# Post-norm vision block on one core: the second attention and the norm behind it, run half by half

## The chip, the cores and the metric

The kernel runs on one core of a Trainium2 chip. The time is the device time of one execution in microseconds (us); the lower, the better. A core has five engines with queues of their own: TensorE (PE in the profile, its weight loads PEld), VectorE (DVE), ScalarE (ACT), GpSimd (POOL) and SyncE (SP, which here only issues transfers). Each works through its own instructions in order and waits for the others at counting semaphores, which the program sets: `wait_ge(sem(name), n)` holds the engine's whole queue until `name` has been raised n times.

## The reference, cut to what matters

Sixteen images of 64 tokens with 64 features pass through a patch embedding, a feed-forward layer, windowed attention with 8 heads, a feed-forward layer, a second attention with one head and a distance bias, a layer norm, and then a block with an RMS norm, rotary attention, an RMS norm and a mixture of 8 experts, and a last layer norm. The change touches the second attention, the layer norm behind it and the RMS norm that opens the next block:

```python
# second attention (one head of 64, bias from two cosines of |i-j| weighted by beta), h3 is its input
q = h3 @ Wq.T + bq; k = h3 @ Wk.T + bk; v = h3 @ Wv.T + bv
o2 = softmax(q @ k.T / 8 + bias) @ v
h4 = layernorm(h3 + o2)                       # (x - m) / sqrt(var + 1e-5)
# third attention opens with an RMS norm of h4, then keys and queries with rotary tables
n = h4 * rsqrt(mean(h4 * h4) + 1e-6) * ln1_w
q3 = rope(n @ wq.T); k3 = rope(n @ wk.T); v3 = n @ wv.T
```

## The kernel before, in words

All activations stay in SBUF. The 1024 tokens stand as 128 rows by 512 columns (two groups of 8 images side by side in the rows). Nearly every step is done twice, once for each half of the columns (g = 0 and g = 1, 256 columns, `HC`), so that one engine can work on one half while the next engine has the other. PSUM is one array of 8 banks, `PS[:, bank, :]`, and half g of the second attention uses banks 4g to 4g+3.

The order of the work is written out by hand, once per engine. In the second attention and the norm behind it each engine does a step for both halves before it goes to the next step:

- TensorE (`block.tensor`, lines 443 to 500): queries and keys (L447, L448) of halves 0 and 1; for each half the bias by a product with the identity (L453) and 8 score products (L459, 64x64 tiles, 16 instructions in the trace); `turn2(0)` (two transposes, L440), the values of both halves (L317), `turn2(1)`; h3 turned and centred for both halves (L470); mixing for both halves (L481); then `stay_awake(15, 1)`, 15 products of zeros into bank 1 whose result nobody reads (L279); the transposes of the normed activations h4n of both halves (L490); and the keys, turned keys, queries and turned queries of the third attention for half 0 and half 1 (L497). Behind them come `values3(0)` (L317 again), a mask product (L505) and `scores3` (L511).
- VectorE (`block.vector`, lines 1155 to 1211): keys' bias (L1157) for both halves, top and shift of the scores (L1162, L1164) for both, values' bias (L1168) for both, reciprocals (L1173), o2 (L1178), sum2 (L1184), sums of squares (L1014), reciprocals of the RMS norm's roots and the scaling to h4n (L1020, L1025), the same for the layer norm (h4), and then the rotary products (L1203) and sums (L1210).
- ScalarE (`block.scalar`, lines 795 to 825): q2 (L799) for both halves, probabilities by Exp (L803) for both, a table load for Sqrt (`bring_table`, L713), squares (L726) for both, roots for the RMS norm (L811) and the layer norm (L719) for both, h4f (L818) for both, a table load for Exp, and the key heads of the third attention (L823).
- GpSimd has nothing in this stretch. Its next work is the sum for q3 (L949). Further on, at the second RMS norm, it takes inverse roots itself: L954 adds the epsilon to 128x4 sums, and L956 raises them to the power -0.5.

h4 (the layer norm's result) is read late, by `open3` and `residual`, behind the third attention's first scores. h4n is read by L490 at once.

Of the kernel before, what the change touches and what calls it, by code (L numbers as in the profile page):

```python
# [30 lines left out]
D = 64  # L31
# [54 lines left out]
def build(nc, x, pack_a, pack_b, pack_c, pack_d, pack_e, out):  # L86
    with ExitStack() as ctx:
# [182 lines left out]
        def _(pe):  # L270
# [172 lines left out]
            pe.wait_ge(sem("pack_c_loaded"), 16)  # L443
            for g in range(2):
                pe.wait_ge(sem("h3_ready"), g + 1)
                cols = slice(g * HC, (g + 1) * HC)
                mm(PS[:, 4 * g, 0:HC], c("aq"), h3[:, cols], start=True, stop=True).then_inc(sem("q2_mm"), 1)  # L447
                mm(PS[:, 4 * g + 1, 0:HC], c("ak"), h3[:, cols], start=True, stop=True).then_inc(sem("k2_mm"), 1)  # L448

            pe.wait_ge(sem("bias_made"), 2)  # L450
            for g in range(2):
# [10 lines left out]
            turn2(0)  # L462
            pe.wait_ge(sem("v2_centred"), 2)
            for g in range(2):
                values(h3, c("av"), D, 4 * g + 2, g).then_inc(sem("v2_mm"), 1)
            turn2(1)

            for g in range(2):
# [4 lines left out]
            for g in range(2):  # L473
# [11 lines left out]

            stay_awake(15, 1)
            for g in range(2):
# [5 lines left out]
            for g in range(2):  # L493
                pe.wait_ge(sem("h4f_ready"), g + 1)
                cols = slice(g * HC, (g + 1) * HC)
                for n, name in enumerate(("fk", "fk_turned", "fq", "fq_turned")):
                    t = mm(PS[:, 1 + 4 * g + n // 2, (n % 2) * HC:(n % 2 + 1) * HC], c(name), h4f[:, cols],  # L497
# [3 lines left out]


# [205 lines left out]
        def _(act):  # L708
# [13 lines left out]
            def squares_of(name, ready, count, src):  # L722

                for g in range(2):
                    act.wait_ge(sem(ready), count[g])
                    f(half(squares, g), half(src, g), ACT.Square).then_inc(sem(name + "_squared"), 1)  # L726

# [66 lines left out]

            act.wait_ge(sem("bias_made"), 2)
            for g in range(2):
                act.wait_ge(sem("q2_mm"), g + 1)

# [6 lines left out]

            bring_table(ACT.Sqrt)
            squares_of("ln1", "ln1_in", (1, 2), sum2)
            for g in range(2):
                at = slice(4 * g, 4 * g + 4)
                act.wait_ge(sem("ln1_sq_sum"), g + 1)  # L810
                f(std_rms[:, at], sq_sums[:, at], ACT.Sqrt, scale=(1.0 + EPS_RMS) / D, bias=const(EPS_RMS * EPS))\  # L811
                    .then_inc(sem("rms1_std"), 1)
            roots("ln1", std, 1.0 / D, EPS)


# [3 lines left out]
            bring_table(ACT.Exp)  # L819
# [125 lines left out]


# [47 lines left out]
        def _(ve):  # L994
# [160 lines left out]
            for g in range(2):  # L1155
                ve.wait_ge(sem("k2_mm"), g + 1)
                v.tensor_scalar(half(k2, g), PS[:, 4 * g + 1, 0:HC], c("abk"), None, ALU.add).then_inc(sem("k2_dve"), 1)  # L1157
            for g in range(2):
# [7 lines left out]
            for g in range(2):  # L1166
# [3 lines left out]
            for g in range(2):  # L1170
                mixed2 = PS[:, 4 * g + 2, 0:4 * (D + 1)].rearrange("q (t d) -> q t d", d=D + 1)
                ve.wait_ge(sem("att2_mixed"), g + 1)
                v.reciprocal(r2[:, 4 * g:4 * g + 4], mixed2[:, :, D]).then_inc(sem("att2_recip"), 1)  # L1173
            for g in range(2):
                ts = slice(4 * g, 4 * g + 4)
                mixed2 = PS[:, 4 * g + 2, 0:4 * (D + 1)].rearrange("q (t d) -> q t d", d=D + 1)
# [3 lines left out]
            for g in range(2):  # L1180
# [6 lines left out]
            for g in range(2):  # L1187
                sum_squares("ln1", g)
            for g in range(2):
                invert("rms1", g, rstd_rms, std_rms)  # L1190
                scale("rms1", g, h4n, sum2, rstd_rms).then_inc(sem("h4n_ready"), 1)
            for g in range(2):
                invert("ln1", g, rstd, std)
            for g in range(2):
# [277 lines left out]
```

## Time and profile before

| | us |
|---|---|
| median of 3 runs | 130.06 |
| lowest, highest | 129.52, 131.12 |
| the profiled execution | 130.09 |
| its span, first to last instruction | 128.3 |
| TensorE, VectorE, ScalarE, GpSimd busy in it | 114.1, 85.2, 62.8, 16.9 |
| mean granted TensorE clock | 0.993 of full speed |

The span is what the trace covers; 1.8 us of the profiled execution's time lie around it. A step that ends the chain later moves the time by the same amount as the span.

### The profile page before, as it was taken

Reading aid. Unit: us, or ns where it says so; the run is one execution under the profiler, and the core shown is the slowest. Engines: PE = TensorE matmul, PEld = TensorE weight load, DVE = VectorE, ACT = ScalarE, POOL = GpSimd, SP = SyncE. Lnnn points to the kernel's source line nnn. Section 1 sums busy time; section 2 is a strip of 40 time slices with the busy share of each in tenths; the row PEclk is TensorE's granted clock in tenths of the full one; section 3 lists DMA queues with packets and bytes.
Section 4 is the critical chain, followed back from the end, with each engine's and each line's share of the span. In section 5 each row is a group of like instructions: output and inputs, shape, how many; then the busy total and the mean of one; then the engine's idle time right before and its main releaser. Section 6 shows DMA issues by size and latency. Waiting matters only on the chain.

```text
span 128.3 us, 2347 instructions
## 1 busy us (share of the span) xinstructions
PE 114.1 (89%) x912; PEld 75.3 (59%) x919; DVE 85.2 (66%) x181; ACT 62.8 (49%) x124; POOL 16.9 (13%) x40
## 2 busy tenths in 40 slices
PE   5999999969999989999999996999999999799630
PEld 2334564737687764795686884878768772224330
DVE  0000599799996354558798644487599949999960
ACT  4000668965132175655853647573575646443040
POOL 7300009300000000000022003270013400000000
PEclk9999999999999999999999999999999999999997
DMA  4999980000000000000000000000000000000003
GB/s 156 331 391 432 418 331 2 0 0 0 5 0 3 5 0 0 3 0 5 0 0 0 5 0 0 5 0 0 0 0 0 0 0 3 0 0 5 0 0 82
DMA packets 2682, 6.99 MB, mean 55 GB/s; under 512 B 1264, under 2 KB 1392, under 8 KB 2544
## 3 DMA queue, kind: packets, MB, share of 16 engines
q1 hardware_dynamic: 2672, 6.86, 14.1%
q8 instruction: 7, 0.11, 0.4%
q14 instruction: 3, 0.02, 0.1%
HBM read 6.59 MB, written 0.26 MB: 53 GB/s over the span
## 4 chain that ended last, share of the span: by engine, by line
PE 59%; DVE 17%; DMA 7%; issue 6%; ACT 4%; POOL 2%; SPq 2%; POOLq 1%; ACTq 0%
DMA shared_x<-x_dram 7%; PE PS L395 5%; PE PS L627 5%; PE PS L628 5%; PE PS L309 4%; PE PS L511 3%; PE PS L381 3%; PE PS L635 3%; PE PS L298 3%; PE PS L372 3%; PE PS L497 3%; DVE shared_x L1338 3%; DVE shared_h L1268 2%; PE PS L405 2%; PE PS L317 2%
## 5 line engine op out<-in xcount | busy, mean ns | idle before, releaser
L1268 DVE TENSOR_TENSOR shared_h<-PS,shared_f 128x512 f32<-128x512 f32 x22 | 14.9, 682 | 5.3 <-ACT shared_f L880 5.2
L627 PE MATMUL PS<-xf,up_hi 128*128 128x512 f32 x44 | 17.8, 404 | 0.3 <-DVE shared_h L1268 0.3
L628 PE MATMUL PS<-xf,up_lo 128*128 128x512 f32 x44 | 17.4, 396 | 0.0
L880 ACT ACTIVATE shared_f<-PS 128x512 f32<-128x512 f32 x22 | 12.9, 595 | 7.3 <-PE PS L628 7.3
L279 PE MATMUL PS<-idle_bf 128*128 128x512 bf16 x34 | 10.7, 438 | 1.8 <-POOL idle_bf L911 1.3
L1104 DVE TENSOR_REDUCE top<-PS 128x8 f32<-128x512 f32 x12 | 8.3, 689 | 2.6 <-PE PS L511 1.2
L627 PEld LDWEIGHTS PS<-xf,up_hi 128*128 128x128 f32 x44 | 8.3, 188 | 2.7 <-DVE shared_h L1268 0.9
L1030 DVE TENSOR_SCALAR kf<-PS,pack_a_sb 128x256 f32<-128x256 f32 x1 | 0.5, 484 | 13.4 <-PE PS L287 13.4
L713 ACT ACT_TABLE_LOAD x7 | 9.0, 1283 | 0.8 <-PEq L1463 0.7
L785 ACT ACTIVATE probs<-PS 128x512 f32<-128x512 f32 x8 | 4.8, 597 | 9.3 <-PE PS L381 9.3
L628 PEld LDWEIGHTS PS<-xf,up_lo 128*128 128x128 f32 x44 | 8.3, 188 | 1.8
L635 PE MATMUL PS<-shared_h,down_w 128*64 128x512 f32 x32 | 8.2, 611 | 1.2 <-DVE shared_h L1330 1.2
L1106 DVE TENSOR_TENSOR shifted<-PS,top 128x512 f32<-128x512 f32 x12 | 8.3, 691 | 0.4
L279 PEld LDWEIGHTS PS<-idle_bf 128*128 128x128 bf16 x39 | 3.8, 106 | 7.5 <-issue 4.0
L287 PE MATMUL PS<-shared_x 128*64 128x256 f32 x48 | 7.4, 435 | 0.3 <-DMA shared_x<-x_dram 0.3
L395 PE MATMUL PS<-vo,probs 128*64 128x18 f32 x128 | 7.2, 214 | 0.0
L395 PEld LDWEIGHTS PS<-vo,probs 128*64 128x64 f32 x128 | 6.4, 137 | 1.2 <-issue 1.2
L949 POOL TENSOR_TENSOR qf<-shared_f 128x256 f32<-128x256 f32 x2 | 1.4, 724 | 43.0 <-DVE shared_f L1203 43.0
L901 ACT ACTIVATE up_w<-PS 128x512 f32<-128x512 f32 x8 | 4.3, 595 | 5.3 <-PE PS L650 5.3
L381 PE MATMUL PS<-pack_a_sb,shifted 128*128 128x128 f32 x32 | 5.2, 285 | 1.2 <-DVE shifted L1106 1.2
L381 PEld LDWEIGHTS PS<-pack_a_sb,shifted 128*128 128x128 f32 x32 | 3.4, 140 | 3.9 <-DVE shifted L1106 3.3
L740 ACT ACTIVATE kf<-PS,pack_a_sb 128x256 f32<-128x256 f32 x1 | 0.5, 473 | 10.8 <-PE PS L287 10.8
(189 smaller groups left out, 217.4 us busy)
## 6 DMA issues: line engine op xcount, KB each, us to landing
shared_x<-x_dram SPq DMA_DIRECT2D x6, 544.0 KB, 6.8
up_w<-pack_d_dram SPq DMA_DIRECT2D x1, 1408.0 KB, 12.5
pack_c_sb<-pack_c_dram SPq DMA_DIRECT2D x1, 796.5 KB, 13.3
pack_b_sb<-pack_b_dram SPq DMA_DIRECT2D x1, 455.0 KB, 9.6
down_w<-pack_e_dram SPq DMA_DIRECT2D x1, 352.0 KB, 13.5
out_dram<-normed SPq DMA_DIRECT2D x4, 64.0 KB, 1.7
pack_a_sb<-pack_a_dram SPq DMA_DIRECT2D x1, 162.0 KB, 9.0
```

Source lines behind the costliest of these rows:

```text
L279: mm(PS[:, bank, 0:cols], idle_bf[:, 0:P], idle_bf[:, 0:cols], start=True, stop=True)
L287: m = mm(PS[HALF * s:HALF * s + HALF, 4 + g, 0:HC], x_sb[:, k, 2 * COLS:XW], x_sb[:, k, first:first + HC], start=(k == 0), stop=(k == KCH ...
L381: t = tp(PS[:, w % 2, ch * P:(ch + 1) * P], shifted[:, w % 2, ch * P:(ch + 1) * P], ident)
L395: t = mm(PS[r, 4 + w // 4, at:at + wide], probs[:, w % 2, col:col + HALF], vo[:, w % 2, (w // 2) * 2 + s, ch].rearrange("q e d -> q (e d)" ...
L627: mm(up, up_hi[:, at:at + P], moving, start=True, stop=False)
L628: mm(up, up_lo[:, at:at + P], moving, start=False, stop=True).then_inc(sem("up_mm"), 1)
L635: t = mm(PS[HALF * s:HALF * s + HALF, bank, tok], down_w[:, DOWN_AT[ch]:DOWN_AT[ch] + D], hh[:, ch, s, tok], start=True, stop=True)
L713: f(table_use[:, :], const(1.0), func)
L880: f(gate[:, n % UPBUF, :], PS[:, UP_BANKS[n % UPBUF][0], :], ACT.Silu).then_inc(sem("gated"), 1)
L1104: v.reduce_max(tops, rows, AX).then_inc(sem(name + "_top"), 1)
L1106: v.tensor_tensor(shifted[:, n % 2, :].rearrange("q (b h n) -> q b h n", b=2, n=N), rows, tops.unsqueeze(3).to_broadcast([P, 2, 4, N]), AL ...
L1268: v.tensor_tensor(hh[:, ch, :, g * HC:(g + 1) * HC], PS[:, UP_BANKS[n % UPBUF][1], :].rearrange("q (s c) -> q s c", s=2), gate[:, n % UPBU ...
```

## The change

Each engine's work on the second attention and the norm is put into functions of one half, and the halves are run some steps apart. The roots and reciprocals of the two norms (two Sqrt activations and two reciprocals for each half) go to GpSimd, which does a multiply-and-add and a power for each norm and half; ScalarE's table loads for Sqrt and back to Exp go with them, and the load for Exp is asked for ahead of q2. `squares_of` is removed. Of the products of zeros, 11 remain in four places.

```diff
 TensorE
-            for g in range(2):
...
-            turn2(0)
-            pe.wait_ge(sem("v2_centred"), 2)
-            for g in range(2):
-                values(h3, c("av"), D, 4 * g + 2, g).then_inc(sem("v2_mm"), 1)
-            turn2(1)
...
-            stay_awake(15, 1)
...
+            pe.wait_ge(sem("pack_c_loaded"), 16)
+            pe.wait_ge(sem("bias_made"), 2)
+            queries_keys2(0)
+            pe.wait_ge(sem("v2_centred"), 2)
+            values(h3, c("av"), D, 2, 0).then_inc(sem("v2_mm"), 1)
+            scores2(0)
+            turn_h3(0)
+            queries_keys2(1)
+            turn2(0)
+            values(h3, c("av"), D, 6, 1).then_inc(sem("v2_mm"), 1)
+            mix2(0)
+            scores2(1)
+            turn_h3(1)
+            stay_awake(1, 1)
+            turn2(1)
+            stay_awake(2, 1)
+            mix2(1)
+            stay_awake(7, 1)
+            turn_h4(0)
+            stay_awake(1, 5)
+            queries_keys3(0)
+            turn_h4(1)
+            queries_keys3(1)
 ScalarE
+            bring_table(ACT.Exp)
             act.wait_ge(sem("bias_made"), 2)
             for g in range(2):
...
             for g in range(2):
                 act.wait_ge(sem("att2_turned"), g + 1)
                 f(p2[:, 2 * g:2 * g + 2, :], PS[:, 4 * g + 1, 0:HC].rearrange("q (u n) -> q u n", n=P),
                   ACT.Exp).then_inc(sem("att2_probs"), 1)
-            bring_table(ACT.Sqrt)
-            squares_of("ln1", "ln1_in", (1, 2), sum2)
-            for g in range(2):
...
-            roots("ln1", std, 1.0 / D, EPS)
+                if g == 0:
+                    act.wait_ge(sem("ln1_in"), 1)
+                    f(half(squares, 0), half(sum2, 0), ACT.Square).then_inc(sem("ln1_squared"), 1)
+            act.wait_ge(sem("ln1_in"), 2)
+            f(half(squares, 1), half(sum2, 1), ACT.Square).then_inc(sem("ln1_squared"), 1)
             for g in range(2):
...
-            bring_table(ACT.Exp)
 GpSimd
+            for g in range(2):
+                at = slice(4 * g, 4 * g + 4)
+                pool.wait_ge(sem("ln1_sq_sum"), g + 1)
+                g_.tensor_scalar(std_rms[:, at], sq_sums[:, at], (1.0 + EPS_RMS) / D, EPS_RMS * EPS, ALU.mult, ALU.add).then_inc(sem("ln1_above"), 1)
+                pool.wait_ge(sem("ln1_above"), 2 * g + 1)
+                g_.tensor_tensor(rstd_rms[:, at], std_rms[:, at], minus_half[:, at], ALU.pow).then_inc(sem("rms1_rstd"), 1)
+                g_.tensor_scalar(std[:, at], sq_sums[:, at], 1.0 / D, EPS, ALU.mult, ALU.add).then_inc(sem("ln1_above"), 1)
+                pool.wait_ge(sem("ln1_above"), 2 * g + 2)
+                g_.tensor_tensor(rstd[:, at], std[:, at], minus_half[:, at], ALU.pow).then_inc(sem("ln1_rstd"), 1)
 VectorE
...
+            keys2(0)
+            values2(0)
+            shift2(0)
+            keys2(1)
+            values2(1)
+            residual1(0)
+            sum_squares("ln1", 0)
+            shift2(1)
+            scale("rms1", 0, h4n, sum2, rstd_rms).then_inc(sem("h4n_ready"), 1)
+            residual1(1)
+            scale("ln1", 0, h4, sum2, rstd)
+            sum_squares("ln1", 1)
+            scale("rms1", 1, h4n, sum2, rstd_rms).then_inc(sem("h4n_ready"), 1)
+            scale("ln1", 1, h4, sum2, rstd)
```

On VectorE `keys2(g)` is L1157, `shift2(g)` L1162 and L1164, `values2(g)` L1168, and `residual1(g)` L1173, L1178 and L1184 in one. On TensorE `queries_keys2(g)` is L447 and L448, `scores2(g)` L453 and L459, `turn_h3(g)` L470, `mix2(g)` L481, `turn_h4(g)` L490 and `queries_keys3(g)` L497, each for one half.

## Rows read from the trace of the kernel before

**Rows 1.** The page: the span, and the chain that ended last, by engine.

```profile
span 128.3 us, 2347 instructions
...
PE 59%; DVE 17%; DMA 7%; issue 6%; ACT 4%; POOL 2%; SPq 2%; POOLq 1%; ACTq 0%
```

**Rows 2.** The chain of waits from 50 to 68 us: start us, us, what.

```profile
50.59 0.63 PE PS L447 x2
...
52.51 0.43 PE PS L453 x2
...
53.55 0.63 PE PS L453 x2
...
54.79 0.37 PE PS L440 x2
...
56.06 0.22 PE PS L440 x2
...
57.17 1.10 PE PS L481 x32
...
58.30 0.18 DVE r L1173
...
59.49 0.43 ACT squares L726
...
61.48 0.44 DVE kf L1025
...
61.96 0.44 PE PS L490 x2
...
62.41 3.72 PE PS L497 x16
...
66.74 1.02 PE PS L511 x16
```

**Rows 3.** The timeline of the same stretch: start us, us, engine, line, operation.

```profile
51.31 0.47 ACT L799 ACTIVATE qf<-PS,q_bias 128x256 f32<-128x256 f32 x1 [1.43 <-PE PS L447]
...
55.20 0.38 ACT L803 ACTIVATE p<-PS 128x256 f32<-128x256 f32 x1 [1.31 <-PE PS L440]
...
56.71 1.28 ACT L713 ACT_TABLE_LOAD   x1
...
58.01 0.20 ACT L713 ACTIVATE table_use<-consts 128x1 f32<-128x1 f32 x1
...
58.41 3.19 PE L279 MATMUL PS<-idle_bf 128*128 128x512 bf16 x14 [0.16 <-issue]
...
62.93 1.28 ACT L713 ACT_TABLE_LOAD   x1
63.58 0.76 DVE L1203 TENSOR_TENSOR shared_f<-PS,pack_c_sb 128x256 f32<-128x256 f32 x2 [0.80 <-PE PS L497]
...
65.55 0.72 POOL L949 TENSOR_TENSOR qf<-shared_f 128x256 f32<-128x256 f32 x1 [41.93 <-DVE shared_f L1203]
```

**Rows 4.** The timeline at the second RMS norm, where GpSimd takes the roots.

```profile
76.81 0.42 DVE L1014 TENSOR_REDUCE sq_sums<-squares 128x4 f32<-128x256 f32 x1 [1.07 <-ACT squares L849]
...
77.32 0.23 POOL L954 TENSOR_SCALAR std_rms<-sq_sums 128x4 f32<-128x4 f32 x1 [9.26 <-DVE sq_sums L1014]
...
77.62 1.04 POOL L956 TENSOR_TENSOR rstd_rms<-std_rms,minus_half 128x4 f32<-128x4 f32 x1
```

**Rows 5.** The timeline where VectorE and GpSimd read SBUF at one time, late.

```profile
84.71 1.04 POOL L960 CAST pick<-pack_c_sb 128x1024 fp32r<-128x1024 f32 x1
...
84.96 1.07 DVE L1225 TENSOR_TENSOR parts<-normed,parts 128x256 f32<-128x256 f32 x1
```

**Rows 6.** GpSimd's own timeline, early, the copy of 8 columns.

```profile
19.64 2.90 POOL L938 CAST router_parts<-router_s 128x8 fp32r<-128x8 f32 x1
```

**Rows 7.** VectorE's own timeline at the same time, an operation with two inputs in SBUF.

```profile
19.33 3.15 DVE L1057 SCALAR_TENSOR_TENSOR up_lo<-up_w,pack_a_sb,up_hi 128x2816 fp32r<-128x2816 f32 x1
```

**Rows 8.** A window of 1 us with little TensorE work: PE, PEld, DVE, ACT, POOL busy, PEclk.

```profile
109.00:110.00 1.00, 0.04 (x2) 0.05 (x2) 1.00 (x3) 0.85 (x2) 0.00 (x0) 1.00 0.00 0
```

More of the change, by code:

```diff
@@ L461, in _, with turn_h3 @@
                 t.then_inc(sem("att2_scores"), 1)
-            turn2(0)
-            pe.wait_ge(sem("v2_centred"), 2)
-            for g in range(2):
-                values(h3, c("av"), D, 4 * g + 2, g).then_inc(sem("v2_mm"), 1)
-            turn2(1)
-            for g in range(2):
+            def turn_h3(g):
                 for u in (2 * g, 2 * g + 1):
@@ L472, in _, with mix2 @@
                 t.then_inc(sem("h3_turned"), 1)
-            for g in range(2):
+            def mix2(g):
                 pe.wait_ge(sem("v2_ready"), g + 1)
@@ L483, in _, with turn_h4 @@
                 t.then_inc(sem("att2_mixed"), 1)
-            stay_awake(15, 1)
-            for g in range(2):
+            def turn_h4(g):
                 pe.wait_ge(sem("h4n_ready"), g + 1)
@@ L491, in _, with queries_keys3 @@
                 t.then_inc(sem("h4_turned"), 1)
-            for g in range(2):
+            def queries_keys3(g):
                 pe.wait_ge(sem("h4f_ready"), g + 1)
-                cols = slice(g * HC, (g + 1) * HC)
                 for n, name in enumerate(("fk", "fk_turned", "fq", "fq_turned")):
-                    t = mm(PS[:, 1 + 4 * g + n // 2, (n % 2) * HC:(n % 2 + 1) * HC], c(name), h4f[:, cols],
+                    t = mm(PS[:, 1 + 4 * g + n // 2, (n % 2) * HC:(n % 2 + 1) * HC], c(name), half(h4f, g),
                            start=True, stop=True)
@@ L720, in roots @@
                         .then_inc(sem(name + "_std"), 1)
[L722 to L726, printed above, removed]
             def gelus(name, u_banks):
@@ L1152, in _, with keys2, shift2 @@
                                        in1=half(h2, g), op0=ALU.add, op1=ALU.add).then_inc(sem("h3_ready"), 1)
-            for g in range(2):
+            def keys2(g):
                 ve.wait_ge(sem("k2_mm"), g + 1)
                 v.tensor_scalar(half(k2, g), PS[:, 4 * g + 1, 0:HC], c("abk"), None, ALU.add).then_inc(sem("k2_dve"), 1)
-            for g in range(2):
+            def shift2(g):
                 ts = slice(4 * g, 4 * g + 4)
@@ L1165, in _, with values2 @@
                                 ALU.subtract).then_inc(sem("att2_shifted"), 1)
-            for g in range(2):
+            def values2(g):
                 ve.wait_ge(sem("v2_mm"), g + 1)
@@ L1169, in _, with residual1 @@
                                 c("abv").unsqueeze(1).to_broadcast([P, 4, D]), ALU.add).then_inc(sem("v2_ready"), 1)
-            for g in range(2):
+            def residual1(g):
+                ts = slice(4 * g, 4 * g + 4)
                 mixed2 = PS[:, 4 * g + 2, 0:4 * (D + 1)].rearrange("q (t d) -> q t d", d=D + 1)
                 ve.wait_ge(sem("att2_mixed"), g + 1)
[L1173 to L1176, printed above, removed]
+                v.reciprocal(r2[:, ts], mixed2[:, :, D]).then_inc(sem("att2_recip"), 1)
                 ve.wait_ge(sem("att2_recip"), g + 1)
@@ L1184, in _ @@
                 v.tensor_tensor(half(sum2, g), PS[:, 4 * g + 3, 0:HC], half(o2, g), ALU.add).then_inc(sem("ln1_in"), 1)
[L1187 to L1194, printed above, removed]
-                scale("ln1", g, h4, sum2, rstd)
+            keys2(0)
[12 more added lines that the diff above has]
+            scale("ln1", 1, h4, sum2, rstd)
             cos = c("rope_cos").unsqueeze(1).to_broadcast([P, 4, N])
```

15 lines of the change are left out of this document (4 added, 11 removed).

## The prediction

> **What bounds the kernel now.** I read the page first: the span is 128.3 us, and the chain that ended last is TensorE for 59% and VectorE for 17% of it [rows 1]. Then I read the chain in order of time around the change, 50 to 68 us [rows 2]. It falls into two parts. From 50.59 to 58.27 TensorE runs without a gap: queries, keys, bias, scores, values and mixing for both halves, each wait of the others covered by the other half's products. From 58.30 to 62.41 the chain leaves TensorE: reciprocal, o2, sum2, squares (59.49), sums, roots, scaling to h4n (half 1's at 61.48), the transposes at 61.96, and at 62.41 the keys and queries of the third attention. In that time TensorE multiplies zeros (14 recorded products from 58.41, 3.19 us, 0.23 each) [rows 3]. Last I read the timeline at 63 to 67 us, for what waits behind: VectorE's rotary products start at 63.58, GpSimd's sum for q3 runs from 65.55 to 66.27 [rows 3], and the scores that need it start at 66.74, because TensorE arrives only then [rows 2]. So VectorE has 66.74 - 66.27 = 0.47 us to spare there, about 0.42 after a handover.
>
> So what the change can win is the 4.1 us of the tail, and it should be judged by when the *second* half leaves it, since the third attention's order needs both halves soon after one another.
>
> **The change part by part.** I lay out the new order with the old durations. The trace gives: 0.43 for a product of 256 columns, 0.63 where it follows 64x64 tiles (52.51 against 53.55), 0.61 for the scores of one half (54.79 - 53.55 - 0.63), 0.22 for two transposes, 0.37 behind tiles and 0.44 on an idle engine, 0.45 for half the values or half of the turned h3 (0.90 between the rows at 54.79 and 56.06, and 0.89 between 56.28 and 57.17, are both halves), 0.55 for mixing one half [rows 2]. A step of VectorE or ScalarE on 128x256 that waits for the one before it takes 0.45 in all (59.49 to 59.94), a reciprocal 0.2 [rows 2], Exp 0.38 [rows 3].
>
> *TensorE, first half.* From 50.59: queries and keys (0.63 + 0.43) to 51.65, values to 52.10, bias and scores to 53.14, turned h3 (0.45 and 0.2 for the change of tile) to 53.79, queries and keys of half 1 to 54.65, turn2(0) to 54.87, values of half 1 to 55.32, mixing of half 0 (0.55) to 55.87. VectorE has half 0's shift done at 54.1 (two steps behind 53.14) and ScalarE's Exp ends at 55.3, both in time. Half 0 is mixed at 55.87, and before that took until about 57.7: 1.8 us earlier.
>
> *TensorE and VectorE, second half.* Bias and scores of half 1 (0.63 + 0.61) end at 57.11, turned h3 at 57.76, one product of zeros at 57.99. VectorE meanwhile does residual1(0): reciprocal, o2, sum2 from 55.9 to 57.0; then `sum_squares("ln1", 0)` waits for ScalarE's square (57.45) and runs to 57.9. Behind that waiting instruction stand the top and shift of half 1, whose scores are there since 57.11; TensorE's turn2(1), Exp, mix2(1) all wait for them. So top and shift end at 58.8 and not at 58.1, and turn2(1) (0.44 on an idle engine) ends at 59.25, Exp at 59.67, mixing at 60.3, where both halves were mixed at 58.27 before [rows 2]: the second half is 2.0 us late. This is the first step that speaks against the change.
>
> *GpSimd's roots.* At the second RMS norm the sum of squares ends at 77.23, GpSimd's add starts at 77.32 (0.23), the power at 77.62 (1.04) and ends at 78.66: 1.43 us from the sums to the inverse root [rows 4]. The old way, root and reciprocal, took 0.55 (60.37 to 60.92, between the rows of rows 2). So every norm and half costs 0.9 more, and the layer norm's follows the RMS norm's in GpSimd's queue: add, handover and power, 1.34 more. The new add also multiplies; no row shows that form, and I bound it by 0.23 (same shape, one operation) and 0.74 (the 0.72 of the sum for q3 on 256 columns, rows 3); I take 0.23, the row of its own shape. The power has no cost of a first call, as its row above was its first.
>
> *The two halves through the tail.* Half 0: sums at 57.9, inverse root at 59.3, h4n at 59.8, against about 61.36 before (half 1's scaling started at 61.48 behind it). Half 1: mixing 60.3, residual1(1) to 61.4, squares and sums to 62.3, root at 63.73, h4n at 64.17, where it was ready at 61.92 [rows 2]: 2.25 us later. The layer norm's root of half 1 comes at 65.07. `scale("ln1", 1)` waits for it, and it stands in VectorE's queue *ahead* of the rotary products, which have nothing to do with it. They start one step later, at about 65.45, where it was 63.58 [rows 3] (pitch 0.35 to 0.38 for two neighbours that do not depend, 0.76 for two). That is 1.87 later, less 0.42 to spare: **+1.45 us** at the scores.
>
> *TensorE's own path.* The seven zero products behind mix2(1) (7 x 0.23) end at 61.9, turn_h4(0) at 62.2, h4f at 62.75 (ScalarE has it behind the square of half 1, which ends at 61.85), and the keys and queries of half 0 run from 62.75 to 64.6 (half of 3.72) and not from 62.41. turn_h4(1) now stands behind them and h4f(1) behind that: 0.22 + 0.5 in which TensorE is idle, where before it ran through. It ends at 67.3 and not at 66.13, +1.15. This is less than VectorE's +1.45, so VectorE's path sets the end. Half 0's head start is lost here: it leaves the tail at 59.8 and is not used before 62.
>
> *Table loads.* The loads at 56.71 and 62.93 (1.28 each) lay beside ScalarE's waiting [rows 3] and win nothing. The new load for Exp starts when ScalarE falls free at 49.88 (51.31 - 1.43) and delays q2(0) to 51.4 to 51.9; TensorE asks for it at 52.10. Cost 0; without that cover (the values ahead of the bias) it would be 0.25. In the trace the use of a table starts 1.30 us after the load does (56.71, 58.01) [rows 3]. The Trainium skill, page "ScalarE: Activation LUTs", section "What ACT_TABLE_LOAD costs", gives 2.66 us for a switch, a drain included; by it q2(0) would be ready at 53.2 and the change would lose another 1.1 us at the scores. The row decides, and I leave it out.
>
> *The reads that VectorE and GpSimd share.* A copy of 8 columns on GpSimd took 2.90 us, from 19.64 to 22.54, beside a VectorE operation with two inputs in SBUF that ended at 22.48 [rows 6, 7]; and a VectorE subtraction with two inputs in SBUF took 1.07 us beside a GpSimd copy that ended at 85.75, 0.28 before it [rows 5], where the same shape takes 0.43 (the scaling of rows 2). So each can hold up the other. The scaling to h4n reads sum2 and the roots, both in SBUF, at the moment when GpSimd starts the layer norm's add. If the add goes first, h4n is 0.2 late; if the scaling then holds the power, the layer norm's root is 0.3 late: +1.75 in place of +1.45. Below, it costs nothing. I take 0.1, nearer to nothing, since GpSimd reads only 4 columns.
>
> Sum: 1.45 + 0.1 = 1.55 on the profiled execution's 130.09 (span 128.3 and 1.8 around it; 0.03 above the median): **131.6 us**. Behind the scores the order is the old one and has no transfer or clock of its own to catch up with, so nothing gives the 1.55 back.
>
> **The rivals.** *The interleaving delivers, no slower than before.* My layout holds half 1 for 0.7 at the sum of squares and charges 0.2 at three changes of tile; if these cost nothing, half 1 is mixed at 59.0. This decides it: TensorE's path is then at -0.15, VectorE's at +0.15, less if the power's 1.04 is partly the engine's own record (its spans are rough). For it: half 0 is 1.8 us earlier and the tail holds no useful TensorE work. Against it: the chain for half 1 is one of dependent steps with durations from rows. 129.9 to 130.5, say 130.2.
>
> *GpSimd holds VectorE through add and power.* If the scaling to h4n has to wait for the whole pair, 1.3 us [rows 4], it does so in both halves. In half 0 it ends at 60.9 and not at 59.8, and residual1(1) starts 0.6 late. In half 1 h4n ends at 66.0: turn 0.44, h4f 0.5, keys and queries to 68.9 or 69.0, +2.8. That gives 132.9. For it: rows 5 to 7. Against it: there is a gap of 0.07 between add and power [rows 4], in which the waiting scaling gets in. The Trainium skill, page "SBUF — State Buffer", section "SBUF: two separate sides", states an exclusive lock for the whole instruction between a VectorE operation with two SBUF inputs and a GpSimd operation that reads SBUF. By that rule, held by one instruction at a time, the sum would be the +1.75 above.
>
> *TensorE's clock falls.* TensorE idles for some 0.8 us before turn2(1) and 0.5 at two more places. For it: more gaps than before. Against it: in the window from 109 us it was busy for 0.04 of 1 us and the granted clock stayed at 1.00, the level of 2.4 GHz [rows 8]. If it fell to 1.2 GHz, the keys' and queries' products alone (3.72) would cost 3.7 more: 135.3.
>
> **How the numbers follow.** Forecast 0.63, interleaving delivers 0.20, GpSimd holds VectorE 0.12, clock 0.05. The forecast's own range is 131.1 to 132.2 (handovers and the 0.3 of the shared reads). The range of 8 in 10 reaches to the rivals on both sides: 130.0 to 132.9. What a measurement of this kernel can tell from no change is about 2%, 2.6 us: above 132.7 lie the clock case and most of the held case, 0.12; below 127.5 only something that I do not see, 0.03; within, 0.85.
>
> **What would show it.** In the profile of the changed kernel: half 0's mixing ends near 55.9 and half 1's near 60.3; VectorE is idle ahead of its sum of squares and TensorE ahead of turn2(1) by some 0.8; the four powers take 1.04 each; h4n of half 1 is ready near 64.2; VectorE waits for GpSimd ahead of h4's second scaling until 65, the rotary products start near 65.4, and the third attention's first scores near 68.2. I am wrong if half 1 is mixed before 59.3, if the rotary products start before 64.3, or if the scores' start moves by less than 0.8 us; a scaling of 1 us or more would speak for the held pair, and a granted clock under 1.00 between 57 and 68 for the last rival.

## The result, and the profile after

The changed kernel takes 133.09 us (median of 4 runs, 132.72 to 133.94) against 130.59 for the kernel before beside it: a ratio of 1.0239, with a 95% interval of 1.0195 to 1.0282. Measured again in a later session it took 132.59 us against 130.21, a ratio of 1.0175 (1.0147 to 1.0204). It is slower by 2.4 to 2.5 us, where 1.55 were forecast, and its median lies just above the range. One execution of run 3 below (136.04 us) was over 1.5% slower than the fastest of its kernel; the ratio in the table leaves it out, the median does not.

| | before | after |
|---|---|---|
| the profiled execution, us | 130.09 | 133.94 |
| its span | 128.3 | 131.9 |
| time outside the span | 1.8 | 2.0 |
| first q2 product to first scores of the third attention | 16.15 | 18.37 |

The last row is the measure for all that follows: the start of the first score products of the third attention minus the start of the first product for q2, 66.74 - 50.59 in [rows 2]. It leaves out how early the input arrived, and the granted clock is 1.00 all through it, in every trace but one.

The page of the changed kernel: the span, the granted clock in forty slices, and the chain that ended last, by engine.

```profile
span 131.9 us, 2342 instructions
...
PEclk9999999999999999999999999599999999999997
...
PE 63%; DVE 19%; issue 6%; POOL 5%; ACT 4%; POOLq 1%; ACTq 0%; DVEq 0%
```

GpSimd now has 5% of the chain, where it had 2% [rows 1]. One slice, at 82.4 to 85.7 us, shows the clock at 0.5; that comes below. The chain of waits of the changed kernel (start us, us, what):

```profile
50.74 0.63 PE PS L445 x2
...
55.48 0.12 issue
55.59 0.70 PE PS L474 x16
...
58.38 0.34 DVE s_top L1173
...
58.75 0.43 DVE s_shift L1175
...
59.23 0.44 PE PS L440 x2
59.67 0.43 PE PS L279 x2
...
60.23 0.70 PE PS L474 x16
...
60.95 0.20 DVE r L1187
...
62.16 0.43 ACT squares L816
...
62.61 0.43 DVE sq_sums L1024
...
63.12 0.21 POOL std_rms L950
...
63.40 1.01 POOL rstd_rms L952
...
64.49 0.44 POOL std L953
...
65.00 1.02 POOL rstd L955
...
66.04 0.42 DVE h L1035
66.46 0.68 DVE shared_f L1216 x2
...
68.33 0.74 POOL qf L959
...
69.11 1.09 PE PS L524 x16
```

Read against [rows 2]. Half 0's mixing (55.59) ends at 56.29, 2.0 us before both halves were mixed in the kernel before (58.27). But the chain does not follow half 0. It goes from half 0's sum of squares (which holds VectorE) to half 1's top and shift at 58.38, over the turn, the Exp (beside it the two zero products) and half 1's mixing, which ends at 60.93. Then it passes through residual, squares and sums to GpSimd at 63.12, and stays on GpSimd through *both* norms (63.12 to 66.02). The layer norm's scaling (66.04) and the rotary products (66.46) follow, and then the scores at 69.11. In the timeline, for the same stretch:

```profile
59.82 0.42 DVE L1035 TENSOR_TENSOR kf<-h,rstd_rms 128x256 f32<-128x256 f32 x1 [0.65 <-POOL rstd_rms L952]
59.87 0.43 POOL L953 TENSOR_SCALAR std<-sq_sums 128x4 f32<-128x4 f32 x1
...
63.32 1.99 PE L487 MATMUL PS<-h,pack_c_sb 128*128 128x256 f32 x8 [0.35 <-ACT h L819]
...
64.44 0.43 DVE L1035 TENSOR_TENSOR kf<-h,rstd_rms 128x256 f32<-128x256 f32 x1 [1.41 <-POOL rstd_rms L952]
64.49 0.43 POOL L953 TENSOR_SCALAR std<-sq_sums 128x4 f32<-128x4 f32 x1
...
65.57 0.47 ACT L819 ACTIVATE h<-PS,pack_c_sb 128x256 f32<-128x256 f32 x1 [2.30 <-PE PS L481]
66.04 0.42 DVE L1035 TENSOR_TENSOR h<-h,rstd 128x256 f32<-128x256 f32 x1 [1.18 <-POOL rstd L955]
...
66.09 1.99 PE L487 MATMUL PS<-h,pack_c_sb 128*128 128x256 f32 x8 [0.57 <-ACT h L819]
```

TensorE's own path: keys and queries of half 0 (the eight products at 63.32), those of half 1 from 66.09, behind a turn and h4f(1) at 65.57. Before, one block of 3.72 began at 62.41 [rows 2].

### The profile page after: what moved, and what is told of

The parts are those of the page before. It is cut to its first block, busy times and chain, and to the rows that moved or that the text cites. A ratio compares the mean times of both kernels' runs of the same rounds, so it can differ in the third digit from the quotient of the medians.

```text
span 131.9 us, 2342 instructions
## 1 busy us (share of the span) xinstructions
PE 116.9 (89%) x915; PEld 76.5 (58%) x915; DVE 85.1 (65%) x177; ACT 59.1 (45%) x117; POOL 23.0 (17%) x48
## 4 chain that ended last, share of the span: by engine, by line
PE 63%; DVE 19%; issue 6%; POOL 5%; ACT 4%; POOLq 1%; ACTq 0%; DVEq 0%
PE PS L287 5%; PE PS L395 5%; PE PS L640 5%; PE PS L279 5%; PE PS L641 4%; PE PS L309 4%; PE PS L524 3%; PE PS L381 3%; PE PS L648 3%; PE PS L298 3%; PE PS L372 3%; DVE shared_x L1351 3%; PE PS L405 2%; DVE shared_h L1281 2%; ACT shared_f L880 2%
## 5 line engine op out<-in xcount | busy, mean ns | idle before, releaser
L279 PE MATMUL PS<-idle_bf 128*128 128x512 bf16 x35 | 11.8, 438 | 1.3 <-POOL idle_bf L911 1.3
L1024 DVE TENSOR_REDUCE sq_sums<-squares 128x4 f32<-128x256 f32 x8 | 3.4, 420 | 3.8 <-ACT squares L849 1.6
```

What stands on the lines that cost most here:

```text
L279: mm(PS[:, bank, 0:cols], idle_bf[:, 0:P], idle_bf[:, 0:cols], start=True, stop=True)
```

## The experiments

Fourteen runs were made; run 9 is the changed kernel once more. "Path" is the 16.15 or 18.37 of the table above, "outside" the time outside the span in all runs of the kernel.

| run | median us | before beside it | ratio (95%) | path | outside |
|---|---|---|---|---|---|
| 1 h4 late | 132.37 | 130.16 | 1.0166 (1.0101 to 1.0231) | 17.96 | 1.98 to 2.06 |
| 2 no power | 132.71 | 130.16 | 1.0188 (1.0138 to 1.0239) | 17.96 | 1.98 to 2.05 |
| 3 power only | 134.92 | 130.16 | 1.0317 (1.0237 to 1.0397) | 20.85 | 2.01 to 2.05 |
| 4 shift first | 132.16 | 130.16 | 1.0160 (1.0111 to 1.0209) | 17.74 | 1.99 to 2.06 |
| 5 old roots | 131.47 | 130.09 | 1.0096 (1.0066 to 1.0125) | 17.57 | 1.74 to 1.82 |
| 6 after, zeros in the gap | 132.44 | 130.09 | 1.0166 (1.0130 to 1.0201) | 18.37 | 1.99 to 2.08 |
| 7 before, zeros in the gap | 130.13 | 130.09 | 0.9992 (0.9972 to 1.0012) | 16.15 | 1.75 to 1.83 |
| 8 half tail | 130.06 | 130.09 | 1.0020 (0.9985 to 1.0054) | 16.14 | 1.75 to 1.82 |
| 9 change again | 132.59 | 130.21 | 1.0175 (1.0147 to 1.0204) | 18.37 | 2.03 to 2.06 |
| 10 both moves | 132.29 | 130.21 | 1.0150 (1.0121 to 1.0179) | 17.42 | 1.99 to 2.12 |
| 11 split pairs | 130.76 | 130.21 | 1.0047 (1.0015 to 1.0080) | 16.81 | 1.76 to 1.83 |
| 12 half tail, 8 zeros | 129.85 | 130.21 | 0.9978 (0.9953 to 1.0004) | 15.87 | 1.74 to 1.82 |
| 13 side powers | 130.70 | 130.14 | 1.0054 (1.0021 to 1.0087) | 16.32 | 2.02 to 2.10 |
| 14 side adds | 130.10 | 130.14 | 0.9980 (0.9958 to 1.0002) | 16.15 | 1.76 to 1.83 |

### 1. The layer norm's scaling out of VectorE's way

```diff
             scale("rms1", 1, h4n, sum2, rstd_rms).then_inc(sem("h4n_ready"), 1)
-            scale("ln1", 1, h4, sum2, rstd)
...
                 t.then_inc(sem("rope_q"), 1)
+                if g == 0:
+                    scale("ln1", 1, h4, sum2, rstd)
```

> The changed kernel, with the layer norm's scaling of half 1 (scale of ln1, 1) moved from ahead of the rotary products to between the rotary products of half 0 and half 1. Theory A (VectorE's queue is held by that scaling, which waits for GpSimd's second power of half 1 until 66.02, and TensorE's own path ends 0.5 to 0.6 us before it): the rotary products start about 1.2 us earlier, near 65.2, but the third attention's first scores only 0.5 to 0.6 us earlier, near 68.5 and not 69.11, because TensorE ends the keys and queries of half 1 at 67.9; 0.5 to 0.6 us less than the changed kernel, so about 2.0 us over the kernel before. Theory B (VectorE alone sets the end): 1.2 us less. Theory C (the wait on VectorE is hidden anyway): no change, 2.5 us over the kernel before.

The path is 17.96, 0.41 less than the change's. The chain now runs over TensorE:

```profile
63.21 2.00 PE PS L487 x8
65.21 0.23 PE PS L481 x2
...
65.46 0.48 ACT h L819
...
65.99 2.00 PE PS L487 x8
...
68.59 1.02 PE PS L524 x16
```

Keys and queries of half 0, the turn, h4f(1), keys and queries of half 1, values, mask, scores: behind half 1's mixing no wait for VectorE or GpSimd is left. So VectorE's queue did set the end (theory A, not C), and TensorE's path was 0.4 us behind it (not B's 1.2).

### 2. GpSimd's power taken away

```diff
-                g_.tensor_tensor(rstd_rms[:, at], std_rms[:, at], minus_half[:, at], ALU.pow).then_inc(sem("rms1_rstd"), 1)
+                g_.tensor_tensor(rstd_rms[:, at], std_rms[:, at], minus_half[:, at], ALU.mult).then_inc(sem("rms1_rstd"), 1)
...
-                g_.tensor_tensor(rstd[:, at], std[:, at], minus_half[:, at], ALU.pow).then_inc(sem("ln1_rstd"), 1)
+                g_.tensor_tensor(rstd[:, at], std[:, at], minus_half[:, at], ALU.mult).then_inc(sem("ln1_rstd"), 1)
```

> The changed kernel with GpSimd's four powers behind the first norm replaced by products of the same operands and shape, so that the norm's factor is another number; all waits and the order stay. It takes the price of the power alone away. Theory A: a product takes 0.2 to 0.3 us and not 1.01, so h4n of half 1 comes 0.8 us earlier and the rotary products 1.5 us earlier, but turn_h4(1) stands behind queries_keys3(0), which ends at 65.2 in both, so TensorE's path stays and the first scores start 0.5 to 0.6 us earlier as in the run before this: 2.0 us over the kernel before. Rival (the powers are the whole loss): 1.6 us less, 0.9 us over the kernel before.

The path is 17.96 again, to the hundredth the same as in run 1, though the products that stand for the powers took 0.20 to 0.26 and h4n of half 1 was there at 63.99. The rival's 1.6 is out. Two different edits that end in one figure show the same bound behind them: TensorE's order.

### 3. The power alone, in the old order

The roots go to GpSimd as in the change, and nothing else is touched:

```diff
-            for g in range(2):
-                at = slice(4 * g, 4 * g + 4)
-                act.wait_ge(sem("ln1_sq_sum"), g + 1)
-                f(std_rms[:, at], sq_sums[:, at], ACT.Sqrt, scale=(1.0 + EPS_RMS) / D, bias=const(EPS_RMS * EPS))\
-                    .then_inc(sem("rms1_std"), 1)
-            roots("ln1", std, 1.0 / D, EPS)
...
```

> The kernel before, its order unchanged, with the roots and reciprocals of the first norm moved to GpSimd as in the change, and the table loads for Sqrt and Exp gone with them. Theory A: GpSimd's queue does the RMS norm and the layer norm of half 0 (2.9 us) before it starts half 1, h4n of half 1 is ready near 65.2 and not 61.9, both transposes stand ahead of the keys and queries on TensorE, and these start 3 us later: 3.0 us over the kernel before, more than the whole change. Rival (the roots are not what costs, the half-by-half order is): less than 1 us over the kernel before.

Path 20.85, 4.7 over the kernel before. In the chain, GpSimd does RMS norm and layer norm of half 0 and then the RMS norm of half 1, one behind the other:

```profile
60.42 0.20 POOL std_rms L940
...
60.70 1.04 POOL rstd_rms L942
...
61.82 0.44 POOL std L943
...
62.33 1.01 POOL rstd L945
...
63.42 0.20 POOL std_rms L940
...
63.70 1.02 POOL rstd_rms L942
...
65.22 0.44 PE PS L490 x2
65.66 5.14 PE PS L497 x16
```

The keys and queries begin at 65.66 and not at 62.41: 3.25 later, where 3.0 were expected. The block then takes 5.14 and not 3.72, which was not expected: from 61.6 to 65.2 TensorE had only two transposes to do, and the granted clock stood at 0.50 from 65.6 to 69. So in the old order GpSimd's roots cost 3.3 us and in this profile the clock 1.4 more. The other executions took 133.25 to 136.04 us, so the clock's share differs from one to the next. In the change GpSimd's work of half 0 (58.48 to 61.39) is over before half 1's sums are there; here it stands ahead of half 1.

### 4. Half 1's shift ahead of half 0's sum of squares

```diff
-            sum_squares("ln1", 0)
             shift2(1)
+            sum_squares("ln1", 0)
+            residual1(1)
             scale("rms1", 0, h4n, sum2, rstd_rms).then_inc(sem("h4n_ready"), 1)
-            residual1(1)
```

> The changed kernel with VectorE's order changed in two places: top and shift of half 1 ahead of the sum of squares of half 0, and residual1(1) ahead of the scaling of half 0 to h4n. Theory A (half 1 is held by the wait for ScalarE's square in VectorE's queue): mixing of half 1 ends 0.8 us earlier, near 60.1 and not 60.93, and all behind it: 0.5 to 0.8 us less than the changed kernel, 1.8 us over the kernel before. Rival (the half-0 chain matters as much, its roots come 0.4 us later): no change.

Mixing of half 1 ends at 60.13 and the path is 17.74, 0.63 less. The wait of VectorE for ScalarE's square, with half 1's finished scores behind it, was a real cost, near the 0.7 of the forecast. The second move in the edit keeps half 0's scaling, whose root now comes at 60.11, out of half 1's way; no run parts the two. One more row of this run is used below: here GpSimd's add for half 0's layer norm has no scaling of VectorE beside it.

```profile
60.19 0.19 POOL L953 TENSOR_SCALAR std<-sq_sums 128x4 f32<-128x4 f32 x1
```

### 5. The order with the old roots

ScalarE's Sqrt and VectorE's reciprocals come back, in the order of run 4 (with one more move: half 1's sum of squares ahead of the layer norm's scaling of half 0); GpSimd has nothing in this stretch. The cut is shown against run 4.

```diff
             shift2(1)
             sum_squares("ln1", 0)
             residual1(1)
+            invert("rms1", 0, rstd_rms, std_rms)
             scale("rms1", 0, h4n, sum2, rstd_rms).then_inc(sem("h4n_ready"), 1)
...
+            bring_table(ACT.Sqrt)
...
+            roots1(0)
             act.wait_ge(sem("ln1_in"), 2)
             f(half(squares, 1), half(sum2, 1), ACT.Square).then_inc(sem("ln1_squared"), 1)
+            features4(0)
+            roots1(1)
+            features4(1)
+            bring_table(ACT.Exp)
```

> The half-by-half order of the change with shift2(1) and residual1(1) moved ahead as in the fourth run, but the roots on ScalarE (Sqrt, its table loaded behind the second Exp) and the reciprocals on VectorE, as in the kernel before; GpSimd has nothing here. It parts the order from GpSimd's roots. Theory A (both cost: GpSimd's latency, and the order, which leaves TensorE idle at half 1's shift and at its turn_h4): h4n of half 1 is ready near 63.7, and TensorE's keys and queries of half 1, behind those of half 0 and one turn, end near 67.4; first scores near 68.0, 0.4 us before the fourth run and 1.3 us behind the kernel before. Rival (the order is sound and GpSimd is all of the loss): the first scores at 66.7 or earlier, no slower than the kernel before.

Path 17.57; 1.4 us over the kernel before, with no GpSimd in it at all. So the order by itself costs more than half of the change's 2.2 us on the path, and the rival (only GpSimd costs) falls. Its chain shows where: half 1's top and shift (57.39 to 58.28) and its turn and Exp (58.33 to 59.2) are dependent steps with too little of TensorE's work left to put beside them, and from 64.82 to 65.60 TensorE does nothing but half 1's turn (0.23) and then waits for h4f.

```profile
57.39 0.44 DVE s_top L1178
...
57.85 0.44 DVE s_shift L1180
...
58.33 0.44 PE PS L440 x2
...
59.33 0.70 PE PS L474 x16
...
62.82 2.00 PE PS L487 x8
64.82 0.23 PE PS L481 x2
...
65.07 0.48 ACT h L826
...
65.60 1.99 PE PS L487 x8
```

### 6, 7 and 9. The clock

Two of the change's first four runs had a mean granted clock of 0.98, and 133.17 and 133.94 us. In the profiled one of them the fall lies behind the gap of 1.2 us ahead of L405, which both kernels have (in the kernel before from 78.6 to 79.8, with the clock at 1.00). Windows of 1 us of the changed kernel (PE, PEld, DVE, ACT, POOL busy, PEclk):

```profile
82.00:83.00 1.00, 0.75 (x14) 0.75 (x16) 0.53 (x2) 0.02 (x1) 0.00 (x0) 0.66 0.00 0
83.00:84.00 1.00, 1.00 (x12) 0.88 (x9) 0.00 (x0) 0.39 (x1) 0.00 (x0) 0.50 0.00 0
84.00:85.00 1.00, 1.00 (x7) 1.00 (x5) 0.57 (x2) 0.38 (x1) 0.00 (x0) 0.50 0.00 0
85.00:86.00 1.00, 1.00 (x5) 0.87 (x4) 0.49 (x2) 0.39 (x1) 0.00 (x0) 0.64 0.08 16
```

The clock stood at 0.50, the level of 1.2 GHz. L405, L574 and L566 there take 1.10, 1.04 and 0.85 in the chain; the same steps in the kernel before (L405, L561, L553), at 1.00, the level of 2.4 GHz, take 0.68, 0.59 and 0.61. With the two products behind them that is about 1.2 us. Run 6 fills this gap in the changed kernel, run 7 in the kernel before:

```diff
             mix3(3)
+            stay_awake(5, 5)
             mixed_to_features("att3", 7, 1)
```

> The changed kernel with five products of zeros into bank 5, which is free there, ahead of mixed_to_features(att3, 7, 1): they stand in TensorE's gap of 1.2 us at 81 to 82.2, behind which the granted clock showed 0.50 for 3.5 us in the changed kernel's profile. Theory D (this gap, and nothing of the change's own stretch, lets the clock fall in some runs, which costs 1.2 us in each of them): no run shows the clock under 1.00 between 82 and 86, runs lie within 0.5 us of each other and the median falls by 0.3 to 0.8 us, to 2.2 us over the kernel before. Rival (the fall follows the thinner stretch at 58 to 66 of the change): it stays in half of the runs.

> The same five products of zeros in the kernel before, as a control; its profile had the same gap at 78.6 to 79.8 with the clock at 1.00. Theory D: runs that fall there are few in the kernel before, so the time is the same to 0.3 us, and its slowest runs (131 us) go. Rival (the fall belongs to the change alone): no run of either kernel without the change ever shows it, no difference at all.

Of the five executions of run 6 four lie within 0.33 us, and the median is 132.44. The fifth, 133.18, is the one with a profile: in it the fall at 82 is gone, and one stands in another place, from 113.8 to 117.2, late in the experts' part. Run 7 changes nothing (0.9992). Run 9 is the unchanged change:

> The changed kernel once more, beside the kernel before in the same session, as the measure for the three that follow and for the first four runs. All theories: 2.4 to 2.9 us over the kernel before, and in about half of the runs a mean granted clock of 0.98 with a time some 0.5 to 1 us above the others.

This time no run lay more than 0.3 us above the others, at 132.36 to 132.65, and the clock in the profile is at 1.00 to the end of TensorE's work. So in one and the same kernel the fall comes in one execution and stays away in another. In the two sessions the medians of the change differ by 0.5 us, but those of the kernel before beside it differ by 0.4 (130.59 and 130.21), so the distance between the two kernels hardly moved: 2.50 and 2.38. The mean clock alone does not tell what a fall costs: in run 9 an execution of 132.53 us has 0.983. Run 6, with the gap filled, is at 2.35. Filling it won nothing that these runs can tell.

The gap stands in all fourteen profiles in which it is not filled, at 1.19 to 1.21 us. The clock falls behind it in five of them: the change, runs 2 and 4, and runs 13 and 14 below, which leave the order and the roots of the kernel before as they are. The clock in run 14's page, in forty slices of 3.2 us:

```profile
PEclk9999999999999999999999999599999999999985
```

So the fall does not need the new order. All five have GpSimd's added instructions, as have four of the nine without a fall; with one profile for each run that is too few to say whether they have a part in it. What tips it is open.

### 10. Both moves together

The edits of runs 1 and 4.

> The two moves of the first and fourth runs together (layer norm's scaling of half 1 behind the rotary products of half 0; shift2(1) ahead of the sum of squares and residual1(1) ahead of the scaling of half 0), GpSimd's powers kept. Theory A (then TensorE's path alone binds: the keys and queries of half 0, one turn, h4f, those of half 1): first scores 17.4 us behind the first product for q2, against 18.4 in the change and 17.6 with the old roots, so GpSimd's powers cost nothing once no queue waits for them; 1.3 us over the kernel before. Rival (each power on the path keeps its price): as in the fourth run, 17.7 and 1.8 us over the kernel before.

The first product for q2 and the first scores in its chain:

```profile
50.72 0.63 PE PS L445 x2
...
68.14 1.02 PE PS L524 x16
```

Path 17.42, by 0.15 *shorter* than with the old roots (17.57), which have a reciprocal of 0.2 on VectorE ahead of half 0's scaling. In the chain of run 10 there is no GpSimd between 50 and 68 us. So GpSimd's 1.01 per power costs nothing here as soon as no queue waits for it; the 2.2 us of the change are 0.95 of queue order on VectorE (of which 0.41 go away with the powers too, in run 2) and 1.27 of TensorE's order. The time (132.29) came out 0.5 above what path and outside give (1.27 + 0.25 over 130.21 is 131.7); its profile has a fall of the clock from 113 to 116.4, which may be worth about that; in the other three executions a fall is only supposed.

### 11. TensorE's order mended

Run 5 with the turn of half 1 between the keys and the queries of half 0 (`pair3(g, 0)` is the keys and turned keys of half g, `pair3(g, 1)` its queries):

```diff
-            queries_keys3(0)
-            turn_h4(1)
-            queries_keys3(1)
+            pair3(0, 0)
+            turn_h4(1)
+            pair3(0, 1)
+            pair3(1, 0)
+            pair3(1, 1)
```

> The fifth run's kernel (half-by-half order, old roots), with turn_h4(1) moved from behind the keys and queries of half 0 to between its keys and its queries, so that ScalarE's h4f(1) runs beside the queries. Theory A (TensorE's idle 0.8 us at that turn is one part of the order's loss): the gap goes, first scores near 16.8 to 16.9 us behind the first product for q2 and not 17.6, 0.6 to 0.7 us over the kernel before. Rival (the fill and drain of the split pairs take it back, or the rotary products set the end): 17.4 or more.

Path 16.81, 0.76 less: TensorE's idle time at that turn is gone, and 130.76 us remain, 0.55 over the kernel before.

### 8 and 12. What half a tail is worth in the old order

The kernel before, with TensorE's scores of both halves together as they were, and half 0 let through first: `mix2(0)` ahead of `turn_h3(0)` and `turn2(1)`, `residual1(0)` and its sum of squares ahead of half 1's, the RMS norm's root of half 0 ahead of half 1's square, the turn of half 1 between keys and queries of half 0, and the layer norm's scalings behind the rotary products of half 0 and behind `shift3(1)`.

```diff
             for g in range(2):
                 values(h3, c("av"), D, 4 * g + 2, g).then_inc(sem("v2_mm"), 1)
+            mix2(0)
+            turn_h3(0)
             turn2(1)
+            turn_h3(1)
+            mix2(1)
...
-            stay_awake(15, 1)
+            stay_awake(11, 1)
...
```

> The kernel before, with what the first runs suggest: TensorE keeps scores of both halves together and mixes half 0 as soon as its values and probabilities are there; VectorE does residual, squares' sum and scaling for half 0 ahead of half 1; roots stay on ScalarE; TensorE turns h4n of half 1 between the keys and the queries of half 0; the layer norm's scalings stand behind the rotary products of half 0 and behind shift3(1). Theory A: mixing of half 0 ends near 56.7 and of half 1 near 58.5, keys of half 0 start near 61.8 and not 62.4, and the third attention's first scores 0.3 to 0.5 us earlier, near 66.3; 0.3 to 0.5 us less than the kernel before. Rival (TensorE's work is one block behind the later half whatever the order): same time as the kernel before to 0.2 us.

No gain (path 16.14): h4n(0) was ready at 60.85 but stood behind the products of zeros, of which 11 were too many. Run 12 has 8 in their place.

> The eighth run's kernel with 8 products of zeros ahead of turn_h4(0) and not 11. In the eighth run h4n of half 0 was ready at 60.85 and TensorE turned it at 61.2 to 61.4, behind the products of zeros. Theory A (these held the path): h4f(0) and the keys of half 0 0.35 to 0.5 us earlier, first scores 15.8 us behind the first product for q2 and not 16.15, 0.3 to 0.4 us less than the kernel before. Rival (the later half holds TensorE whatever comes ahead): no difference.

Path 15.87, keys of half 0 from 61.89. 129.85 us against 130.21, the lowest median of all kernels; but the interval (0.9953 to 1.0004) still holds 1, so it beats the change surely and the kernel before only by the trace. Its chain now goes over ScalarE's table load for Sqrt (L722, 1.28 us from 58.48), which the kernel before hid: here GpSimd's roots might have a place. No run tries it.

### 13 and 14. What lies outside the span

In every run of every kernel with GpSimd's roots 1.98 to 2.12 us lay outside the span, and 1.74 to 1.84 in every other. Run 13 puts the eight GpSimd instructions into the kernel before, on tiles that nobody reads; run 14 only the four multiply-and-adds.

```diff
+            for g in range(2):
+                at = slice(4 * g, 4 * g + 4)
+                pool.wait_ge(sem("ln1_sq_sum"), g + 1)
+                for n in range(2):
+                    g_.tensor_scalar(side[:, at], sq_sums[:, at], (1.0 + EPS_RMS) / D, EPS_RMS * EPS, ALU.mult, ALU.add).then_inc(sem("side_above"), 1)
+                    pool.wait_ge(sem("side_above"), 2 * g + n + 1)
+                    g_.tensor_tensor(side_root[:, at], side[:, at], minus_half[:, at], ALU.pow).then_inc(sem("side_done"), 1)
+                    pool.wait_ge(sem("side_done"), 2 * g + n + 1)
```

> The kernel before, with the change's eight GpSimd instructions (four multiply-and-adds, four powers) added at the same place on tiles that nobody reads; roots stay on ScalarE. Nobody waits for them. Theory E (the eight instructions by themselves lengthen the part of the time outside the span, which was 1.98 to 2.12 us in every run of a kernel that has them and 1.74 to 1.83 in every other): outside the span 2.0 to 2.1, 0.25 us over the kernel before; first scores 16.15 us behind the first product for q2 as before, up to 0.3 later if VectorE's scalings are held up. Rival (what lies outside the span follows the removed table loads or the other order, not these instructions): 1.75 to 1.83 outside the span, no change in the time.

> The same with the four multiply-and-adds alone, no powers. Theory E with the cost by the number of GpSimd's instructions: between 1.83 and 2.0 outside the span. Rival (it comes with the powers): 1.75 to 1.83; rival (it is a step that comes with any): 2.0 to 2.1.

Run 13: 2.02 to 2.10 in all ten runs. Run 14: 1.76 to 1.83 in all eleven. So the 0.25 comes with the added instructions and not with the table loads that went. Run 2, with products for powers, had it too (1.98 to 2.05), so it isn't the power. Four multiply-and-adds don't bring it and eight instructions do; since the four that run 14 lacks are also the ones with two input tensors, the runs don't tell the number from the kind. What happens there, before the first or behind the last recorded instruction, no trace shows; that it goes by the length of GpSimd's program is a supposition. In run 13 the sum for q3 starts only at 66.01, behind the last power, and the path is 0.17 longer: the eight instructions are not quite free, though nobody reads their results.

## Why the prediction was wrong in size

The direction, the place and the order of the bounds held; the size did not: 1.55 us forecast, 2.4 to 2.5 measured. On the path it is 2.22 for 1.55: 0.59 from the second half's sums, 0.14 from the shared reads, less 0.07 for a shorter root, and 0.02 behind the rotary products; each is taken up below. Then 0.25 lie outside the span. And the kernel before, from whose 130.09 us the forecast was counted, stood at 130.59 beside the change. Together that is 133.06; the median was 133.09.

*TensorE, first half.* The forecast had half 0 mixed 5.28 us behind the first q2 product (55.87); it was 5.55. One half's mixing by itself takes 0.70 and stands 0.12 behind its waits, where half of the pair's 1.10 had been put in. This is the first mis-sized term, and half 1's mixing pays it again.

*TensorE and VectorE, second half.* The hold at `sum_squares("ln1", 0)` is there (run 4: 0.63). Half 1 was mixed 10.19 us behind the first product, forecast 9.71. Of these 0.48, 0.27 are carried on from half 0; nearly all the rest is half 1's own mixing, 0.84 from the Exp's end (60.09) to 60.93 for 0.63. The residual then took 1.21 and not 1.1. Together the sums of half 1 were 0.59 later than forecast: **the failed step is the layout of the second half through mixing and residual**, in which durations of steps that ran in pairs were halved or taken without their handovers.

*GpSimd's roots.* 1.36 us from the sums (63.04) to the root (64.40), forecast 1.43; the new add with its product took 0.20, near the 0.23 taken from the row of its own shape.

*The shared reads.* Forecast 0.1, measured 0.24. The layer norm's add took 0.43 beside VectorE's scaling, which reads two tensors in SBUF, at 59.87 and 64.49 in the timeline above, and ended just behind it. In run 4, where no such instruction of VectorE ran beside it, half 0's took 0.19 (at 60.19). GpSimd waited and VectorE did not (the scaling kept its 0.42 to 0.43), so the held rival (h4n at 66.0) did not come: h4n(1) was there at 64.87. That the rival's 132.9 lies near the measured 133.09 is chance. The other direction is in run 13: there GpSimd's sum for q3 (66.01, 0.72) began just before VectorE's sum for k3 (66.03), which took 0.98 and not the 0.43 that it takes in the kernel before. The Trainium skill, page "SBUF — State Buffer", section "Who interferes with whom", says that a VectorE instruction with two SBUF inputs contends with a GpSimd instruction that reads SBUF, that the lock is an exclusive one, and that issue order decides who blocks. By that rule the add would wait out the scaling that began before it, and the trace agrees, with 0.43 against 0.19.

*The layer norm's scaling ahead of the rotary products.* Right: VectorE waited until 66.02, and the rotary products began at 66.38, 15.64 us behind the first product, forecast 14.86; the difference of 0.78 is the 0.59 above, 0.24 of the shared reads and 0.07 less for the root, to 0.02. The 0.42 to spare behind them was 0.4.

*TensorE's own path.* Right in its place and its rank. It was 1.81 over the kernel before and not 1.15 (run 1). Of these 0.66, 0.47 are the same late second half, and 0.15 are half 0's keys and queries, which took 2.00 by themselves where half of the block's 3.72 had been put in; VectorE's path lay 0.41 beyond it, forecast 0.3. The forecast put this path behind VectorE's and asked no further; yet 1.27 of the 2.22 stay when every queue is cleared (run 10). That share is TensorE's order, and GpSimd has no part in it.

*Table loads.* Right: q2(0) ran from 51.47 to 51.94, TensorE's bias product began at 52.24 in the chain, and nobody waited. The load took 1.28 from 50.05, and its use began at 51.34, 1.29 after the load's start and not 2.66.

*The rest.* 0.25 us lie outside the span (runs 13 and 14), on which the forecast had no row. The second session's 132.59 would have lain within the range and the first's 133.09 does not; the 0.5 between them is mostly one of sessions, as the kernel before moved by 0.4 with it, and not a matter of the mechanism. The forecast's own range, 131.1 to 132.2, missed both.

*The rivals.* The interleaving did not deliver: half 1 was mixed at 60.93 (60.78 on the forecast's time), not at 59.0, and run 5 has the interleaving without GpSimd at 1.4 us over the kernel before. The clock fell behind a gap that both kernels have, not in the change's own stretch from 50 to 69 us, where it stayed at 1.00.

## What to carry to other kernels

A tail is over when its *second* half leaves it: an interleaving pays only if each of the second half's dependent steps has products of the first half beside it, and a lone step costs more than half of a pair (0.70 for a lone mixing, against 0.55; 2.00 for a lone block of keys and queries, against 1.86). Before a step is moved to a slower engine, look less at its duration than at who stands behind its waiter: GpSimd's powers cost 3.3 us where half 1 queued behind half 0, 0.4 where the rotary products queued behind a scaling that nobody needed yet, and nothing measurable in TensorE's order once the moves of runs 1 and 4 were made.

## What the runs showed of the hardware

- On GpSimd a power on 128x4 took 1.01 to 1.04 us, twice more (1.06 in run 3, 1.20 in run 13), and a product of the same shape 0.20 to 0.26 (run 2).
- A multiply-and-add on GpSimd that reads 4 columns took 0.43 beside a VectorE instruction with two inputs in SBUF that had begun just before it, and 0.19 without (runs 4 and 10). A VectorE sum that began just behind one of GpSimd took 0.98 and not 0.43 (run 13).
- Eight more GpSimd instructions, whose results nobody reads, add 0.25 us outside the span (run 13); four multiply-and-adds add none (run 14).
- Behind one and the same gap of 1.2 us of TensorE the granted clock stayed at 1.00 in nine profiles and fell to 0.50 in five, for some 3.4 us in the change's; behind 3.6 us with only two transposes (run 3) it was at 0.50 for about as long. The changed kernel itself shows both: a fall in its first profile, none in run 9.
